# Second stage of a Mamba and FFN layer: silu and gelu at state 4, the copy of the sum at state 6, and what hangs on them moved to match

## The reference, cut to what matters

```python
xn = layernorm(x)                                   # x: 4 x 512 tokens x 512
proj = Win @ xn;  hs, gate = halves of proj         # 1024 channels each
hs = silu(causal_conv4(hs) + bconv)
dt_in, Bm, Cm = split(Wx @ hs);  dt = softplus(Wdt @ dt_in + bdt)
for each channel d, state n of 16:                  # scan over the 512 tokens
    h[t] = exp(A[d, n] * dt[d, t]) * h[t-1] + dt[d, t] * Bm[n, t] * hs[d, t]
    y[d, t] += h[t] * Cm[n, t]
y = (y + hs * D) * silu(gate);  attn = Wout @ y
ffn = fp8(gelu(fp8(xn) @ fp8(wg0)) * (fp8(xn) @ fp8(wg1))) @ fp8(w_linear)
out = x + attn + ffn                                # bf16 results between the FFN's steps
```

## Time and profile before

| | |
|---|---|
| median of 3 runs | 1261.31 us (1261.01 to 1263.42) |
| profiled execution | 1263.65 us; its span from first to last instruction 1261.9 us |
| mean granted TensorE clock | 0.901 of full |
| busy over the whole span | DVE 84%, POOL 77%, PE 77%, ACT 60% |
| ScalarE's table switches | 31 units with silu, 20 of them with gelu |

### The profile page before, as it was taken

How to read it: one execution, slowest core, us unless ns; L and a number is a source line. 1 busy time by engine, 2 the same in 40 slices (tenths; PEclk the granted TensorE clock), 3 DMA queues, 4 the chain that set the end, 5 groups by cost and what they waited for, 6 DMA issues and landing times.

```text
span 1261.9 us, 16993 instructions
## 1 busy us (share of the span) xinstructions
PE 965.4 (77%) x4304; PEld 577.9 (46%) x4304; DVE 1056.4 (84%) x1205; ACT 760.7 (60%) x1097; POOL 977.0 (77%) x783
## 2 busy tenths in 40 slices
PE   4888888467668787877677878776778787767888
PEld 3655555143344454444344544433445444434554
DVE  7877966588888998888789988887889888888994
ACT  4878786565666465666555655665546566656451
POOL 4342433698888799888788998887879988889792
PEclk9999999788888898988788988897879898889899
DMA  8665768861111137211111372111112721111100
GB/s 281 213 236 197 262 239 318 307 240 46 51 34 55 34 99 281 77 61 64 45 55 34 117 262 80 63 59 45 55 34 99 281 75 61 67 42 34 34 1 34
DMA packets 51603, 147.38 MB, mean 117 GB/s; under 512 B 5680, under 2 KB 14000, under 8 KB 48432
## 3 DMA queue, kind: packets, MB, share of 16 engines
q1 hardware_dynamic: 51504, 146.26, 33.2%
HBM read 108.23 MB, written 38.01 MB: 116 GB/s over the span
## 4 chain that ended last, share of the span: by engine, by line
POOL 51%; issue 20%; PE 4%; DVE 3%; ACT 2%; POOLq 1%; DVEq 0%
POOL dbu L920 38%; POOL hp L928 13%; DVE hp L974 1%; PE yT L1095 1%; PE mm L1053 1%; DVE da L974 1%; PE mm L1017 1%; DVE prod L943 1%; PE da L1017 1%; ACT L867 1%; ACT L863 1%; PE mm L1074 0%; POOLq L919 0%; ACT gate_bf L867 0%; ACT L868 0%
## 5 line engine op out<-in xcount | busy, mean ns | idle before, releaser
L879 ACT ACTIVATE da<-unit,neg_a 128x512 f32<-128x512 f32 x512 | 340.9, 686 | 354.8 <-DVE prod L943 344.5
L920 POOL TENSOR_TENSOR dbu<-unit,b_head 128x512 f32<-128x512 f32 x384 | 490.0, 1303 | 10.6 <-issue 5.8
L974 DVE TENSOR_TENSOR_SCAN da<-da,dbu 128x512 f32<-128x512 f32 x320 | 381.3, 1217 | 3.3 <-POOL dbu L920 2.3
L1095 PE MATMUL yT<-ident,prod 128*128 128x128 f32 x1280 | 225.1, 305 | 97.9 <-DVE prod L943 97.4
L974 DVE TENSOR_TENSOR_SCAN hp<-da,dbu 128x512 f32<-128x512 f32 x192 | 232.5, 1211 | 77.0 <-PE yT L1095 62.3
L928 POOL TENSOR_TENSOR hp<-hp,c_head 128x512 f32<-128x512 f32 x160 | 204.1, 1275 | 109.9 <-DVE hp L974 109.9
L1095 PEld LDWEIGHTS yT<-ident,prod 128*128 128x128 f32 x1280 | 163.2, 155 | 240.4 <-DVE prod L943 210.3
L1053 PE MATMUL mm<-xn_b,wffn 128*128 128x512 fp8e4 x512 | 160.0, 452 | 26.1 <-DVE acc L961 10.1
L920 POOL TENSOR_TENSOR dbu<-unit,b_all 128x512 f32<-128x512 f32 x128 | 160.1, 1275 | 0.0
L943 DVE TENSOR_TENSOR prod<-da,c_head 128x512 f32<-128x512 f32 x224 | 148.9, 665 | 0.0
L1095 PE MATMUL yT<-ident,hp 128*128 128x128 f32 x768 | 126.8, 292 | 0.0
(11 more groups left out here) (106 smaller groups left out, 1328.5 us busy)
## 6 DMA issues: line engine op xcount, KB each, us to landing
unit<-unit_d SPq DMA_DIRECT2D x32, 768.0 KB, 4.4
unit_d<-dt_du SPq DMA_DIRECT2D x32, 512.0 KB, 2.7
wf<-in_wffn SPq DMA_DIRECT2D x12, 1024.0 KB, 6.0
c_head<-bc_d SPq DMA_DIRECT2D x24, 512.0 KB, 5.4
b_head<-bc_d SPq DMA_DIRECT2D x18, 512.0 KB, 5.2
unit_d<-hsd SPq DMA_DIRECT2D x32, 256.0 KB, 4.0
wffn<-w_d SPq DMA_DIRECT2D x64, 128.0 KB, 3.9
wgate<-in_win_gate SPq DMA_DIRECT2D x32, 256.0 KB, 4.1
```

The costliest lines, as they stand in the source:

```text
L879: nc.scalar.activation(da[n % SLOTS][:, :], unit[:, k % 2, 0, :], ACT.Exp, scale=neg_a[:, k, n:n + 1]).then_inc(da_ready, 1)
L920: nc.gpsimd.tensor_tensor(dbu[:, n % DBUS, :], unit[:, k % 2, 1, :], b_all[n // NS][:, n % NS, :], ALU.mult).then_inc(dbu_ready, 1)
L974: nc.vector.tensor_tensor_scan(state, da[n % SLOTS][:, :], dbu[:, n % DBUS, :], 0.0, ALU.mult, ALU.add).then_inc(scanned, 1)
L1095: ins = nc.tensor.matmul(yT[k % 2][:, t * P:(t + 1) * P], product[:, t * P:(t + 1) * P], ident[:, :], start=False, stop=last, is_transpose ...
```

## The change

Silu and gelu go from n=6 to n=4, the copy of the sum stays at n=6 as a step of its own (`SUM`), the transpose back goes from n=2 to n=4, the gating from n=6 to n=7, the gelu product from n=4 to n=5 (it was at 5 in k=5) and so the clamp from 5 to 6, the FFN copies from 7 to 8, and some places of the gate, out and lin groups and copies move by one to three.

```diff
-SWITCH = 6
+SWITCH, SUM, GATED = 4, 6, 7
-FFN, FFN_COPIED = (3, 2, 2, 2, 2), (7, 7, 7, 7, 7)
+FFN, FFN_COPIED = (3, 2, 2, 2, 2), (8, 8, 8, 8, 8)
-GATE = (12, 9, 9, 9, 11, 11, 11, 9)
-OUT_A_LIN = {4: (), 5: (("out_a", 0, -3), ("lin", 0, 5), ("out_a", 1, 8)),
+GATE = (12, 9, 9, 9, 11, 12, 11, 9)
+OUT_A_LIN = {4: (), 5: (("out_a", 0, -3), ("lin", 0, 7), ("out_a", 1, 9)),
-LIN_COPIED = {(5, 12): 0, (6, 11): 1, (6, 15): 2, (7, 12): 3}
-GELU_USED = (4, 4, 4, 4, 5)
-BACK = 2
+LIN_COPIED = {(5, 15): 0, (6, 12): 1, (6, 15): 2, (7, 13): 3}
+GELU_USED = (5, 5, 5, 5, 5)
+BACK = 4
...
                         nc.scalar.preload_act_table_set("natural_log_exp_and_others")
+
+                    if n == SUM and not first:
                         sum_of(u - 1, before)
...
-                    if n == 6 and not first:
+                    if n == GATED and not first:
                         gated(u - 1, (k - 1) % KU)
```

## The result

| | before | after |
|---|---|---|
| median of four runs beside one another | 1261.70 us (1261.01 to 1263.42) | 1302.99 us (1300.97 to 1305.11) |
| profiled execution, its span | 1263.65, 1261.9 us | 1305.11, 1303.3 us |
| mean granted TensorE clock | 0.901 | 0.899 |

The ratio is 1.0325 (95% interval 1.0305 to 1.0346). The change makes the kernel slower by 41.3 us. The sign of the forecast is right; its size, +85 us to 1346, is not: less than half of it came. The time lies inside the stated range (1296 to 1376) only because its lower end was the first rival's time. The place where most of the difference lies is the forecast's step 3.

A forecast was written before the change was run, and what follows sets the result against it. VectorE's own work plus its waits around ScalarE's table switch bound a unit's length. Terms 74 + 9 + 2 - 9 + 7 + 2 = +85 us on the 1261.31 median gave about 1346 us, range 1296 to 1376.

The forecast's parts named there:

- the first rival: Gelu product gets in after one GpSimd instruction: 2.4 us less in 20 units, -48, 1298 us; chance 0.12.
- step 3: Gelu product behind scan 5 waits until GpSimd stops, 3.8 us behind scan 5's end, ending at E3 + 11.0.
- Step 1: Silu, gelu and table loads before exp 4: new 3.5 us wait before scan 4 in k=1 to 4; gelu's 2.63 goes.
- Step 2: Scan 4, state 3's product with c, then scan 5 take 2.9 us; scan 5 ends at E3 + 6.4.
- E3: The end of scan 3 in a unit, from which the forecast measures to the start of scan 7.
- Step 4: Scan 6 and the clamp in k=1 to 4: 1.15 + 0.95 us, the clamp ending at E3 + 13.1.
- Step 5: Clamp, FFN copy, third FFN group, adds, scan 7: uncovered chain of 4.3 us; scan 7 starts at E3 + 17.4.
- Other units: Outside k=1 to 4: k=5 +9 us, k=6 and 7 +2, k=0 -9; k=4's later FFN copies +7, k=1 to 3's +2.
- the +16 kept in the range: Lin and out_a moves in k=5 to 7: bank delays priced zero; 1.3 us in 12 units if cover failed.
- Full clock: Chain from clamp to scan 7 takes 2.9 us instead of 4.3 in 16 units: -22, 1324 us; chance 0.08.
- Faster: Scan 7's wait comes from the transpose back, not the clamp's chain: about 1231 us; chance 0.05.
- It cancels: Product in the gap, chain at its shortest, TensorE's freed n=2 used in all units: under 1265 us; chance 0.02.

The follow-up runs named there:

- The second experiment: Kernel before with the gelu product at state 5 and the clamp at 6 in all units, nothing else moved: 1295.13 us, ratio 1.0257.
- eighth: Bench without the layer: VectorE asks for the product in GpSimd's third or thirteenth of 20 multiplies; 0.96 to 2.07 us, against 9.4 to 10.4 in 15 of 16.
- ninth: Bench asking in GpSimd's 2nd to 18th of 20 multiplies: 1.20 to 1.66 us up to the 12th, then 3.84 to 10.06; with a pause before the ninth multiply, 0.96 to 2.03.
- thirteenth: Kernel of experiment 7 with one GpSimd wait added ahead of dbu 4: 1202.01 us, ratio 0.9537.
- the benches: Runs without the layer: VectorE asks for a product or clamp while GpSimd runs six or twenty multiplies; products took 0.96 to 2.07 us or 3.84 to 10.4.
- experiments 4: Changed kernel with the gelu product back at 4 (5 in k=5), the clamp at 5 and the FFN copies at 7: 1282.24 us, ratio 1.0146.
- 6: FFN groups from place 4, gate groups behind them: changed kernel 1224.37 us, ratio 0.9695; kernel before, copies also at 8, 1231.17 us, ratio 0.9752.
- 5: Kernel before with silu and gelu alone at state 4, the copy of the sum left at 6: 1269.46 us, ratio 1.004.
- The third experiment: Changed kernel with silu and gelu back at state 6, all else left as changed: 1303.49 us, ratio 1.033.
- experiment 7: Changed kernel with FFN groups from place 4, gate groups behind, silu and gelu at 5, product at 4 (5 in k=5): 1203.58 us, ratio 0.9547.
- experiment 12: Kernel of experiment 7 with GpSimd multiplying hp of state m behind dbu m+2 instead of m+3: 1205.69 us, ratio 0.9547.

## Why the prediction was right in sign and wrong in size

- **Step 1, right.** 3.5 us before scan 4 in k=1 to 4, 3.9 in k=5, 0.7 in the others were forecast, 79 us in all; measured 3.50 in 16, 3.93 in 4, 0.71 in 11, 80.3 in all. The waits for gelu went.
- **Step 2, right.** E3 to the end of scan 5 is 6.45 us (6.4 forecast) in the unit shown.
- **Step 3, wrong; this is the step that failed.** It made the product wait for GpSimd's stop, ending 11.0 us behind E3. It got in at the next boundary in 20 of 20 units, 1.06 to 1.93 us long, and in k=1 to 4 ended 8.6 behind. 2.4 us in 16 units is 38 us; with k=5's (forecast +2.3 a unit, measured about +0.4) it comes to 46 us, where the total missed by 43; what is left went the other way in small terms below. The rows that it rested on, k=5 and the first unit, were read rightly, but what set them apart was not seen. There GpSimd had been at work for 19 and 31 instructions without a pause. In the new order it has just been held for scan 5 (2.2 us in most units, 0.14 in the first), a wait that the text of step 3 itself names. The second experiment shows that step 3's behaviour is real, and the eighth, ninth and thirteenth when it comes. The right answer would have been the first rival, 1298 us, which was given 0.12.
- **What the rival rested on.** The Trainium skill (SBUF — State Buffer, section "Who interferes with whom") says that a VectorE instruction with two inputs in SBUF contends with a GpSimd one that reads SBUF, and that whoever issues first has the shared pair of ports for the whole instruction. From that the rival had the product held for one GpSimd instruction at most. The kernel after agrees in 20 of 20, and so do the benches' asks up to the twelfth instruction. The benches' asks from the thirteenth on, 3.8 to 10.4 us but for one of 1.88, go against it; there the measurements decide.
- **Step 4, right.** Clamp 0.94 us in k=1 to 4; 0.95 was forecast. The wider one of k=5 took 1.78, not the 1.2 forecast.
- **Step 5, right.** 4.47 us from the clamp's end to scan 7, with the clock at half; 4.3 was forecast. It is what makes the change slow (experiments 4 and 6). Over the 16 units it is 4.2 to 4.5 us in 14 and 2.8 in two.
- **Other units.** k=0: the waits of 3.4 to 4.2 us at scan 7 went, but for 1.3 in one batch. k=4's scan 12 waits 2.2 us, as forecast (0.47 + 1.7). k=1 to 3 have 0.5 there, 0.2 was forecast. A cost priced at nothing came, but small: in k=5 scan 12 waits 1.5 to 2.7 us for its buffer where it waited 0.3 to 2.0 before, 3 us more in the four units (that `lin` 0, moved to place 7, is the cause was not tested; the +16 kept in the range covered it).
- **The rivals.** "Full clock": refuted, the clock is 0.50 in the chain. "Faster" through the transpose back: refuted by the same chain, and by experiments 4 and 5: the wait for `hp` is 59.0 us with the transpose back left at 2 and 69.8 with it at 4. "It cancels": two of its three conditions did not hold.

The third experiment adds a warning on reading the sum: with the switch left at 6 the terms are others (waits for the exponential of 2.3 us in all, products of 4.4 us and more in k=1 to 3) and the total is the same to 0.5 us. That a total fits would not have shown the terms right.

What stays open: why the line lies at about the thirteenth instruction, whether it goes by instructions or by time (all GpSimd instructions here begin about 1.22 us apart, and 15.0 to 16.0 us is the thirteenth), and why near it the same ask is now short and now long. That experiment 7 shows both kinds after a pause of 0.19 us is such a case of the edge and says nothing against short pauses: 0.03 to 0.14 us started the count anew elsewhere. Whether the clamp, with one input in SBUF, ever waits for the end of a run was not tried that late.

## What to carry to other kernels

Ask of an instruction on a shared path not only what stands beside it but how long the other engine has been running when it is asked for: rows of two units that differ in that can't be carried over to each other. Before moving a consumer later, follow what hangs on it through buffers and banks on other engines; here the chain clamp, copy, third FFN group, add, scan held VectorE for 80 us, and other places for two kinds of matmul groups took it away. And when a change has several parts, run the parts: the one that gave its name to this one (the switch) cost 6 of the 41 us when made alone.

## What the runs showed of the hardware

- VectorE's product with two bf16 inputs in SBUF got in at GpSimd's next boundary (0.96 to 2.07 us with its own work in the benches) while GpSimd was in the 1st to 12th instruction since it last stood idle. From the 13th to the 18th of 20 it waited for the end of the whole run, 3.8 to 10.4 us, but for the earliest ask in the 13th (1.88 us); GpSimd's instructions pass in front of it. In the layer the line is less sharp: both kinds came 15.8 to 16.0 us after the run began.
- One pause of GpSimd starts the count anew, even a very short one: 1.3 and 0.14 us in the bench, 0.31 and 0.1 us in the layer, and 0.03 and 0.04 us in two asks of experiment 12.
- While the product has its turn, GpSimd is the one delayed: two `dbu` with product and clamp between them took 3.97 us instead of 2.5.
